# A stage's closing stores awaited later, and the next stage's first loads, ones and identity moved into it

## What is computed

```
t = t + _L2_ffn_ref(_ln_t(t), ...)      # two experts of eight
t = t + _L3_attn_ref(_ln_t(t), L3_attn_w_qkv, L3_attn_w_proj)
...
qkv = x @ w_qkv;  q, k, v = split(qkv)   # 12 heads of D = 16
att = softmax((q @ k.T) * D ** -0.5);  y = att @ v;  return y @ w_proj
```

## Time and profile before

| | |
|---|---|
| median of 3 runs | 1116.69 us (1114.40 to 1118.52) |
| the profiled execution | 1116.58 us, its span 1114.7 us |
| TensorE busy, mean granted clock | 991.8 us (89%), 0.931 of full speed |
| VectorE, ScalarE, GpSimd busy | 578.7, 419.9, 282.8 us |
| stage l3p | about 812.5 to 874.0 us of the span |
| stage l3a | from 874.47 us |

### The profile page before, as it was taken

The page is one execution under the profiler, slowest core; times in us unless marked ns, Lnnn a source line. Parts: engine busy times, 40 slices in busy tenths (PEclk is TensorE's granted clock), DMA queues, the critical chain, the costliest instruction groups (busy, mean ns, idle before and its releaser), DMA issues. The chain is left out here.

```text
span 1114.7 us, 20465 instructions
## 1 busy us (share of the span) xinstructions
PE 991.8 (89%) x7510; PEld 752.8 (68%) x7511; DVE 578.7 (52%) x1396; ACT 419.9 (38%) x853; POOL 282.8 (25%) x397
## 2 busy tenths in 40 slices
PE   5998999999699999999799469999959799993996
PEld 5796888887375887787698426666647445572675
DVE  3844755552321565655666733444368477744221
ACT  3755254545223242444350011111127266641332
POOL 4663401010200121100001334555412211103242
PEclk9976999999899999999898679999969899995998
DMA  5455753310011320000007311112144433415760
GB/s 93 105 156 154 183 145 81 92 44 2 3 43 64 89 48 1 23 1 1 1 2 215 106 36 43 51 46 50 31 135 107 125 117 90 144 44 186 206 207 13
DMA packets 103318, 91.58 MB, mean 82 GB/s; under 512 B 25905, under 2 KB 95095, under 8 KB 102590
## 3 DMA queue, kind: packets, MB, share of 16 engines
q1 hardware_dynamic: 93221, 77.20, 25.2%
q0 software_dynamic: 5632, 11.07, 3.7%
q10 hardware_dynamic: 4377, 2.12, 0.7%
HBM read 64.44 MB, written 29.70 MB: 84 GB/s over the span
## 5 line engine op out<-in xcount | busy, mean ns | idle before, releaser
L1358 DVE TENSOR_REDUCE l0a_nmax<-l0a_psS 98x2 f32<-98x392 f32 x96 | 54.3, 566 | 40.8 <-PE l0a_psS L1175 32.8
L2904 ACT ACTIVATE l2e_H<-l2e_psH 128x512 f32<-128x512 f32 x40 | 21.7, 594 | 130.3 <-PE l2e_psH L2866 130.3
L921 ACT ACTIVATE l3a_PT<-l3a_psST 128x512 f32<-128x512 f32 x96 | 54.6, 595 | 31.8 <-PE l3a_psST L832 31.1
L1308 ACT ACTIVATE l0a_PT<-l0a_psST 98x392 f32<-98x392 f32 x96 | 47.2, 497 | 42.2 <-PE l0a_psST L1217 41.8
L2884 PEld LDWEIGHTS l2e_psY<-W2T,l2e_HT 128*128 128x128 f32 x320 | 51.4, 190 | 16.1 <-issue 15.9
L2827 POOL DMA_INDIRECT ys<-l2e_Y,result_of x40 | 42.0, 1050 | 72.4 <-DVE l2e_Y L2931 66.3
L2884 PE MATMUL l2e_psY<-W2T,l2e_HT 128*128 x320 | 57.3, 332 | 1.5 <-DVE l2e_Y L2931 0.8
L967 DVE TENSOR_REDUCE l3a_nmax<-l3a_psS 128x2 f32<-128x512 f32 x48 | 33.0, 687 | 25.0 <-PE l3a_psS L802 25.0
L2931 DVE COPY l2e_Y<-l2e_psY 128x384 f32<-128x384 f32 x20 | 11.2, 558 | 65.4 <-PE l2e_psY L2884 65.4
L2863 PE MATMUL l2e_psH<-W1T,l2e_XT 128*128 x80 | 41.3, 640 | 2.8 <-issue 2.0
L2822 POOL DMA_INDIRECT l2e_X<-xn,token_at x40 | 39.2, 980 | 17.2 <-issue 17.2
(11 more groups left out here) (591 smaller groups left out, 2698.6 us busy)
## 6 DMA issues: line engine op xcount, KB each, us to landing
l3w_A<-in_w SPq DMA_DIRECT2D x8, 771.0 KB, 4.7
l3w_B<-in_w SPq DMA_DIRECT2D x8, 672.0 KB, 5.5
l3a_QS<-qd SPq DMA_DIRECT2D x72, 64.0 KB, 2.2
l3a_KS<-kd SPq DMA_DIRECT2D x72, 64.0 KB, 2.3
rd<-l0r_p SPq DMA_DIRECT2D x24, 168.0 KB
first_QS<-qd SPq DMA_DIRECT2D x54, 64.0 KB
first_KS<-kd SPq DMA_DIRECT2D x54, 64.0 KB
W2T<-in_w2t SPq DMA_DIRECT2D x2, 1536.0 KB, 16.5
```

What stands on the lines that cost most here:

```text
L921: nc.scalar.activation(PT[n % 3][:, s, :], psST[item % 2][:, :], ACT.Exp).then_inc(exp_done, 1)
L1308: ex = nc.scalar.activation(PT[n % 3][0:WQ, s, :], psST[item % 2][0:WQ, 0:2 * W0], ACT.Exp)
L1358: mx = nc.vector.tensor_reduce(nmax[k % 2][0:WQ, 2 * j:2 * (j + 1), s], psS[item % 2][0:WQ, 0:2 * W0].rearrange("p (t k) -> p t k", t=2), ...
```

## The change

The tiles QS, KS and identb, and the piece tiles of l3p with the semaphores of their stores, now belong to an outer stage (l3q, class FullFront) that lasts over both stages. Into l3p go the 16-bit identity (ScalarE, first), the ones (GpSimd, after the third image's statistics), and the loads of groups 0, 1 and 2 (SyncE, six transfers behind each image's stores from the third image on, after a wait for the stores of images 0 and 1). SyncE no longer waits for the last stores in l3p but in l3a, ahead of group 9. l3a loses its eight products; l3p has nine products of 512 columns ahead of its first transposes and five behind its last product. At the start VectorE normalises image 0 before it takes the statistics of image 1. The class PositionPieces of the first attention is rewritten on the same base without a change in what it does.

```
+class LastingPieces:
+    def __init__(self, st, name, prt, n, dims, units, dmas=1):
+        self.n, self.units, self.unit = n, units, 16 * dmas
+        self.tiles = [st.sb(f"{name}{u}", [prt, 3, *dims], BF16) for u in range(n)]
+        self.out = [st.sem(f"{name}_out{u}") for u in range(n)]
+    def finish(self, eng):
+        for u in range(self.n):
+            eng.wait_ge(self.out[u], self.unit * (len(range(u, self.units, self.n)) + 1))
+
+class FullFront:
+    def __init__(self, st):
+        self.nc, self.ring = st.nc, 4
...
+        self.q, self.k = (LastingPieces(st, name, CH, 2, (2, T), B) for name in "qk")
...
+    def clear_ones(self, pool):
+        for k in range(self.ring):
+            if k:
+                pool.wait_ge(self.ones_done, k)
+            self.nc.gpsimd.memset(self.KS[k][SR:QR, :, :], 1.0).then_inc(self.ones_done, 1)
+    def load(self, sp, G, k, tiles, src, terms):
+        p, g, slot = k // HG, k % HG, k % self.ring
+        term_rows(sp, tiles[slot], src, (p * 3 * C + g * GQ * HD) * 2 * T, terms, self.stack_in[slot])
...
 def full_attention (l3a)
         def _(sp):
...
-            for k in range(NK):
-                load(k)
+            for k in range(HG, NK):
                 if k >= ring:
                     sp.wait_ge(t_full, 8 * (k - ring + 1))
+                if k == (NP - 1) * HG:
+                    front.q.finish(sp)
+                    front.k.finish(sp)
+                front.load_queries(sp, G, k)
+                front.load_keys(sp, G, k)
...
             pool.wait_ge(stats.pow_done, 1)
-            for k in range(ring):
-                if k:
-                    pool.wait_ge(ones_done, k)
-                nc.gpsimd.memset(KS[k][SR:QR, :, :], 1.0).then_inc(ones_done, 1)
-            pool.wait_ge(ones_done, ring)
...
-            pe.wait_ge(ident_done, 1)
-            for c in range(8):
-                nc.tensor.matmul(psS[0][:, 0:NH * 32], G["ident"][:, :], V[:, c, :, :].rearrange("p h d -> p (h d)"), start=True, stop=True)
...
-            nc.scalar.activation(identb[:, :], G["ident"][:, :], ACT.Copy).then_inc(ident_done, 1)
...
 def combined_inputs (l3p)
             for i in range(B):
                 for pieces, dst in ((qp, G["qd"]), (kp, G["kd"])):
                     pieces.sync(...)
-            qp.finish(sp)
-            kp.finish(sp)
+                if i == 2:
+                    for pieces in (qp, kp):
+                        for u in range(2):
+                            sp.wait_ge(pieces.out[u], 2 * pieces.unit)
+                if i >= 2:
+                    (front.load_keys if i % 2 else front.load_queries)(sp, G, i // 2 - 1)
...
                 stats.gpsimd(nc, pool, i, i % 2)
+                if i == 2:
+                    pool.wait_ge(stats.kept, i + 3)
+                    front.clear_ones(pool)
+                    pool.wait_ge(front.ones_done, front.ring)
...
+            for c in range(9):
+                nc.tensor.matmul(psQ[:, :], G["ident"][0:CH, :], W[:, 0, 0:512], start=True, stop=True)
             turn(0)
             for i in range(B):
                 project(i)
+            for c in range(5):
+                nc.tensor.matmul(nm.psT[0][:, :], G["ident"][0:CH, :], W[:, 0, 0:512], start=True, stop=True)
...
+            nc.scalar.activation(front.identb[:, :], G["ident"][:, :], ACT.Copy).then_inc(front.ident_done, 1)
             nm.scalar(nc, act, 0, 0)
...
-                stats.vector(nc, dve, i, i % 2, (added, 2 * TI * (i + 1)))
+
+            def stat(i):
+                stats.vector(nc, dve, i, i % 2, (added, 2 * TI * (i + 1)))
...
             combine(0)
+            stat(0)
             combine(1)
             norm(0)
+            stat(1)
             for i in range(B):
...
                     combine(i + 2)
+                    stat(i + 2)
```

More of the change, by code:

```diff
@@ L689, in keep, with load_queries, load_keys, full_attention @@
         sp.dma_start(rows(xn, row0 * 2 * C, [2 * C, P], [P * 2 * C, 4], [1, C]), self.XN[:, tiles, :]).then_inc(self.xn_kept, 16)
-def full_attention(nc, G, stats_eps, router):
+class LastingPieces:
[9 more added lines that the diff above has]
+        self.nc, self.ring = st.nc, 4
+        self.QS, self.KS = ([st.sb(f"{name}{k}", [QR, GQ, 2 * T], BF16) for k in range(self.ring)] for name in ("QS", "KS"))
+        self.identb = st.sb("identb", [P, P], BF16)
+        self.q, self.k = (LastingPieces(st, name, CH, 2, (2, T), B) for name in "qk")
+        self.stack_in = [st.sem(f"stack_in{k}") for k in range(self.ring)]
+        self.ones_done, self.ident_done = st.sems("ones_done ident_done")
+    def clear_ones(self, pool):
[6 more added lines that the diff above has]
+        term_rows(sp, tiles[slot], src, (p * 3 * C + g * GQ * HD) * 2 * T, terms, self.stack_in[slot])
+    def load_queries(self, sp, G, k):
+        self.load(sp, G, k, self.QS, G["qd"], Q_TERM)
+    def load_keys(self, sp, G, k):
+        self.load(sp, G, k, self.KS, G["kd"], K_TERM)
+def full_attention(nc, G, stats_eps, router, front):
     with Stage(nc, "l3a") as st:
@@ L701, in full_attention @@
         W2 = 2 * T
-        ring, lead = 4, 4
-        QS = [st.sb(f"QS{k}", [QR, GQ, W2], BF16) for k in range(ring)]
-        KS = [st.sb(f"KS{k}", [QR, GQ, W2], BF16) for k in range(ring)]
+        ring, lead = front.ring, 4
+        QS, KS, identb, stack_in, ones_done = front.QS, front.KS, front.identb, front.stack_in, front.ones_done
         PT = [st.sb(f"PT{k}", [P, GQ, W2]) for k in range(3)]
@@ L719, in full_attention @@
         psA, psB = st.ps("psA"), st.ps("psB")
-        stack_in, rows_in = [st.sem(f"stack_in{k}") for k in range(ring)], [st.sem(f"rows_in{k}") for k in range(ring)]
+        rows_in = [st.sem(f"rows_in{k}") for k in range(ring)]
         s_full, max_done, split, split_done, m_turned, m_copied = st.sems("s_full max_done split split_done m_turned m_copied")
         t_full, exp_done, av_done, o_copied, grouped, inverted, norm_done = st.sems("t_full exp_done av_done o_copied grouped inverted norm_done")
-        o_turned, ot_done, y_full, x_added, ident_done, ones_done = st.sems("o_turned ot_done y_full x_added ident_done ones_done")
+        o_turned, ot_done, y_full, x_added = st.sems("o_turned ot_done y_full x_added")
         block = st.block()
@@ L1020, in term_rows @@
         sp.dma_start(dst[t * HD:(t + 1) * HD, :, :], rows(src, at + piece * C * 2 * T, [2 * T, HD], [HD * 2 * T, GQ], [1, 2 * T])).then_inc(sem, 16)
-class PositionPieces:
+class PositionPieces(LastingPieces):
     def __init__(self, st):
[L1028 to L1035, removed]
+        super().__init__(st, "p", HB * WS, 3, (1, FOUR * T), FOURS * 4, 3)
 def position_rows(sp, G, RS, k, sem):
@@ L3178, in _, with combined_inputs @@
                 combine(e)
-def combined_inputs(nc, G, eps, rows_out):
+def combined_inputs(nc, G, eps, rows_out, front):
     with Stage(nc, "l3p") as st:
@@ L3187, in combined_inputs @@
         stats, nm = LnStats(st, G, eps), Normed(st, G)
-        qp, kp = Pieces(st, G, "q", CH, (2, T)), Pieces(st, G, "k", CH, (2, T))
+        qp, kp = Pieces(st, G, "q", CH, (2, T), lasting=front.q), Pieces(st, G, "k", CH, (2, T), lasting=front.k)
         psQ, psK = st.ps("psQ"), st.ps("psK")
@@ L3442, in full_attention @@
             G = dict(self.G, VA=ctx.enter_context(self.nc.sbuf_tensor("Vall3", [P, NT, NH, 32], F32)))
-            combined_inputs(self.nc, G, 1e-5, rows_out)
-            full_attention(self.nc, G, 1e-5, front)
+            lasting = FullFront(ctx.enter_context(Stage(self.nc, "l3q")))
+            combined_inputs(self.nc, G, 1e-5, rows_out, lasting)
+            full_attention(self.nc, G, 1e-5, front, lasting)
     def one_expert(self, out, front):
```

6 lines of the change are left out of this document (removed).

## The result

The changed kernel takes 1110.38 us (median; 1103.85 to 1119.31), the kernel before 1116.75 on the same chips: ratio 0.9949, 95% interval [0.993, 0.9968]. It is faster by 6.4 us where 10.9 were forecast; the time lies inside the range, at its upper end (0.9949 of the 1116.69 of before would be 1111.0, the end itself). The profiled execution has a span of 1108.5 us (1114.7 before), 6.2 less.

The account below looks back on a forecast made before the run. TensorE fills the l3a loop, so the time is at l3p's edges. First score 9.1 us sooner (KF's 1.26 included) plus 1.85 for row waits make 10.9: 1116.6 becomes 1105.7 us, range 1102 to 1111.

Parts of the forecast that it names:

- What bounds the kernel: The l3a loop keeps TensorE busy 95.36 of 98.70 us at full clock; the time is at l3p's edges.
- nothing stands before the first score: Head of l3a: rows, ones and identity are ready; first score at about 873.3 instead of 882.39, 9.1 us gained.
- Part 1: Opening of l3p: nine products raise the clock in 5.2 us, end at 822.84; KF of image 0 gains 1.26 us.
- so the gain reaches its end: l3p after KF: VectorE and TensorE pace the stage as before, so the 1.26 us arrives at its end.
- So I let the moved ones cost VectorE nothing: l3p: GpSimd's memsets of ones, 7.37 us, do not slow VectorE's normalisations; cost 0.
- first rival: l3p, about 831.5: a memset holds up VectorE's normalisation, 1.8 us once or twice, 1107.5 to 1109.3; chance 0.07.
- the sixth group: End of l3p: six loads behind the last store take 2.7 us, replacing the 2.8 us wait; SyncE still ends last.
- I take it as warm: Start of l3a: TensorE has stood 1.7 us, less than the 4.0 after which the clock fell, so scores run warm.
- third rival: Hand-over to l3a: the clock falls, first scores run at 1.2 GHz, at most 2.6 us lost, 1108.3; chance 0.06.
- Part 3, the rows: l3a: three waits for rows go, 1.85 us gained; group 4 may give back up to 0.76, not counted.
- Rivals 2, 4 and 5: Opening products don't lift the clock in time (0.08); SyncE's issues become the bound (0.04); max rows come last in l3a's head (0.04).
- The forecast's own case: All terms as forecast: 10.9 us gained, 1105.7 us; chance 0.71.

Follow-up runs that it names:

- the version without the hold: Changed kernel with two of the four memsets of ones moved to the start of l3p: 1109.22 us, ratio 0.9932.
- the combined kernels: Changed kernel, three memsets early, five opening and three closing products, group 2's keys in l3a: 1100.66 us; also five slots 1099.60; also no closing products 1102.63.

## Why the prediction was right and wrong

**What bounds the kernel:** right. The time was at the edges of l3p; what lies behind l3a takes as long as before (104.42 us from its first load to the end of the span, 104.13 before).

**Part 3, "nothing stands before the first score":** right, and it is the gain. The first score follows l3a's start by 0.04 us; put the eight products back and the kernel before's time is back.

**Part 1:** the mechanism was right as far as KF. In the profiled execution the rise took 6.0 us, not 5.2, so the nine products ended at 823.9 instead of 822.84 (0.28 of it the later start of the stage), and KF gained 0.58, not 1.26. Other executions with the same nine products gained up to 1.41 on the one profile of before, so neither 5.2 nor 1.26 was a bad guess. What failed is "so the gain reaches its end": the last store, 58.38 us after the stage's start before, stood at 58.60 to 58.91 in the six rows in which the ones had not been moved from behind the third statistics and nine products opened the stage. What the step saw and did not follow to its end is that products beyond the rise only stand in the way: it named the early normalisation as bought for nothing, and with five products KF comes some 2.3 to 3.6 us sooner than with nine.

**Part 2, the first step that failed:** "So I let the moved ones cost VectorE nothing". The hold took 0.93 us in the profiled execution and 1.4 to 2.0 in five others with the same opening, as much as KF had gained and more, because it ends with the memset: in these six, with KF between 15.20 and 16.03 us, the pair ended 21.15 to 21.48 us after the stage's start. The prediction had the mechanism as its first rival, for 1.8 us and a chance of 0.07, and set it aside on one row that it read as six undisturbed normalisations of 128x192; three of them were 128x64, and the six were 0.29 us late. The Trainium skill ("SBUF — State Buffer", "Who interferes with whom") says that of a VectorE instruction in a two-port mode and a GpSimd instruction the one that issues first has the shared ports for the whole instruction, and the other stands; the runs agree, in both directions (0.34 us on VectorE's side, 0.08 on GpSimd's, beside 97x576), and the price up to one memset for each normalisation was borne out with five opening products (2.65 us held).

**Part 2, the sixth group:** right that SyncE still ends the stage and that awaiting the stores later gains nothing (0.13). The size was off: six issues took 3.45 us there, 2.65 in the quiet head of l3a, and "2.7 for the wait of 2.8" became 0.59 more in the hand-over.

**Part 3, the second step that failed:** "I take it as warm". TensorE stood 2.24 us, not 1.7, and the clock fell 3.5 us after the last closing product although scores ran by then. The third rival had this, at up to 2.6; it cost 1.1. The distance of 4.0 us between products and fall was that of one execution and no safe limit: in the nine profiles in which TensorE stood for 2.08 to 3.04 us the clock fell 1.65 to 4.3 us after the last product, in three of them before TensorE had begun again. The four with 0.30 to 0.46 us of standing kept it.

**Part 3, the rows:** the waits went, as put, and group 4 gave back 0.88, a little over its bound of 0.76, which had been left out of the sum; the 0.41 at group 6 had not been seen at all.

**Rivals 2, 4 and 5** did not come: the clock rose, the loads inside l3p did not delay the stores (the last store of the version without the hold is 0.78 us sooner than before), and the max rows held up nothing. The row of the second rival, from 74 to 84 us, was not all of 112 columns: 32 of its 63 products had 16.

**The range** held by luck. The forecast's own case, with 0.71, did not come, and neither did its bounds of 1103.1 to 1107.6; rivals 1 and 3, with 0.13 between them, came both, and the range reached 1111 because its upper end was set at them. Of the signs named, the end of l3p behind 874 came (SyncE's last issue ended at 875.28), and so did the long normalisation.

## What to carry to other kernels

An idle engine is not free for any work: GpSimd's memset is to be laid where VectorE does not normalise, and a row that looks undisturbed is read with its shapes kept apart and from both sides, the memset's duration too. Products that keep the clock up are counted to the point where the next real work is ready, at the front no more than fit before it, at the back enough to reach it. When work is moved ahead of a boundary, the last piece of it is the one to leave behind: six issues moved back over it gave more here than any other single edit.

## What the runs showed of the hardware

- Exclusion of VectorE's normalisation (fp32 TENSOR_SCALAR) by a memset is by whole instructions and goes both ways: pairs of 0.66 us became 1.00 beside memsets of 0.58, and 1.59 to 3.31 beside memsets of 1.84. VectorE's subtractions (TENSOR_TENSOR) kept their 0.68 to 0.69 beside the same memsets, and its fill of 2.46.
- After a standing of 2.08 to 3.04 us the clock fell 1.65 to 4.3 us behind the last dense fp32 product, also when 16-bit score products had been running for up to 2.1 us by then. In the head of l3a the fall costs 0.9 to 1.0 us in seventeen maxima where the clock was low for 3.4 us, and 1.7 to 1.8 where it was low for 6.8. The rise came 4.3 to 6.0 us after the opening products began, in twelve profiles of the same products.
- The fall at the end of l3a comes 10.6 to 13.2 us after the last products with the values in twelve profiles and 3.3 to 3.5 in two, in one of these for good, at some 4 us; no row that was read tells the cases apart.
- Six issues on SyncE took 2.65 to 2.77 us at the head of l3a and 3.29 to 3.45 at the end of l3p, where the DMA share is 0.70 (870 to 876; 0.42 from 876 to 877); in the combined kernels, at the head of l3a but right behind the last store, the first six took 2.96 to 3.07.
